# A Mamba recurrence that begins with four input projections done instead of six, and makes five a step instead of three

## The reference

```
zxbcdt = x @ in_proj_w.T            # z 1024 | xv 256 | B 256 | C 1024 | dt_in 128
dt  = softplus(dt_in @ dt_proj_w.T + dt_proj_b)        # 1024 channels
dA  = exp(dt[..., None] * A);  dBx = (dt * x_full)[..., None] * Bg   # 16 states each
h_t = dA_t * h_(t-1) + dBx_t ;  y_t = sum over states of C_t * h_t
y   = (y + D_skip * x_full) * silu(z)  ->  out_proj
```

## Time and profile before

| | us |
|---|---|
| median of 3 runs | 2858.53 (2854.5 to 2859.29) |
| the profiled execution | 2856.02 |
| its span | 2854.2 |
| VectorE, TensorE, POOL, ScalarE busy in it | 2129.0, 2650.3, 1256.3, 1152.0 |
| first scan of step 0 begins | 77.13 |

### The profile page before, as it was taken

The page is one execution under the profiler, slowest core; times in us unless marked ns, Lnnn a source line. Parts: engine busy times, 40 slices in busy tenths (PEclk is TensorE's granted clock), DMA queues, the critical chain, the costliest instruction groups (busy, mean ns, idle before and its releaser), DMA issues.

```text
span 2854.2 us, 32450 instructions
## 1 busy us (share of the span) xinstructions
PE 2650.3 (93%) x11096; PEld 1884.4 (66%) x11096; DVE 2129.0 (75%) x2731; ACT 1152.0 (40%) x1690; POOL 1256.3 (44%) x836
## 2 busy tenths in 40 slices
PE   7888888888888878999999999999999999999999
PEld 3444444444444327888887777888877888888887
DVE  4999999999999985653366677778767865556553
ACT  5555555555455534432244443443333422222221
POOL 2789888988889971210000023223312522222220
PEclk8888998989889869999999999999999999999999
DMA  6654654554465527221111112112111121111111
GB/s 232 210 158 119 188 163 122 151 174 126 120 192 149 149 82 244 94 74 49 48 67 60 45 37 67 45 45 67 45 38 45 45 52 45 52 49 48 51 46 67
DMA packets 152309, 275.35 MB, mean 96 GB/s; under 512 B 27344, under 2 KB 27856, under 8 KB 151632
## 3 DMA queue, kind: packets, MB, share of 16 engines
q1 hardware_dynamic: 152144, 273.27, 32.3%
HBM read 178.01 MB, written 61.34 MB: 84 GB/s over the span
## 4 chain that ended last, share of the span: by engine, by line
PE 70%; DVE 11%; ACT 8%; issue 4%; POOL 3%; DMA 2%; SPq 1%; DVEq 0%; POOLq 0%; ACTq 0%
PE ps L1733 18%; PE ps L1734 18%; PE ps L1735 18%; PE ps L1772 8%; DVE state L1358 5%; ACT ps L847 5%; PE ps L1784 4%; POOL read L1172 2%; DMA vpack<-vl 1%; PE ps L1924 1%; DVE act_o L1677 1%; PE ps L1868 1%; DMA uraw<-y_d 1%; PE ps L1898 1%; DVE drive L1349 1%
## 5 line engine op out<-in xcount | busy, mean ns | idle before, releaser
L1172 POOL TENSOR_TENSOR read<-state,c_t 128x512 f32<-128x512 f32 x512 | 664.3, 1310 | 134.9 <-DVE state L1358 115.9
L1358 DVE TENSOR_TENSOR_SCAN state<-ps,drive 128x512 f32<-128x512 f32 x512 | 624.8, 1220 | 13.1 <-ACT ps L847 11.5
L1733 PE MATMUL ps<-xh,ghi 128*128 128x512 f32 x1536 | 608.3, 396 | 0.0
L1231 POOL TENSOR_TENSOR wdeq<-packed,scales 128x1024 f32<-128x1024 f16 x96 | 260.3, 2711 | 789.1 <-DVE packed L1510 789.1
L1735 PE MATMUL ps<-xh,glo 128*128 128x512 f32 x1536 | 599.0, 390 | 0.0
L1734 PE MATMUL ps<-xl,ghi 128*128 128x512 f32 x1536 | 598.7, 390 | 0.0
L847 ACT ACTIVATE ps<-ps,a_exp 128x512 f32<-128x512 f32 x512 | 338.8, 662 | 470.6 <-PE ps L1772 468.9
L1772 PE MATMUL ps<-dpack,sel 128*128 128x512 f32 x512 | 261.4, 511 | 110.7 <-DVE state L1358 109.3
L1677 DVE TENSOR_TENSOR act_o<-act_o,ps 128x512 f32<-128x512 f32 x192 | 131.7, 686 | 306.1 <-PE ps L1735 290.3
L1349 DVE TENSOR_TENSOR drive<-ps,b_t 128x512 f32<-128x512 f32 x512 | 346.3, 676 | 11.9 <-PE ps L1772 11.4
L1099 ACT ACTIVATE ahi<-act_o 128x512 fp32r<-128x512 f32 x192 | 121.4, 632 | 562.2 <-DVE act_o L1677 562.2
(11 more groups left out here) (204 smaller groups left out, 3782.6 us busy)
## 6 DMA issues: line engine op xcount, KB each, us to landing
whi<-w_d SPq DMA_DIRECT2D x63, 256.0 KB, 4.1
wlo<-w_d SPq DMA_DIRECT2D x63, 256.0 KB, 4.9
dpack<-dh SPq DMA_DIRECT2D x64, 128.0 KB, 3.8
dpack<-dl SPq DMA_DIRECT2D x64, 128.0 KB, 3.5
b_d<-ev SPq DMA_DIRECT2D x32, 256.0 KB
x_d<-ev SPq DMA_DIRECT2D x32, 256.0 KB, 2.6
vpack<-vh SPq DMA_DIRECT2D x64, 128.0 KB, 3.4
vpack<-vl SPq DMA_DIRECT2D x64, 128.0 KB, 2.6
```

Source lines behind the costliest of these rows:

```text
L1172: pool.tensor_tensor(read[:, n % RRING, :], state[:, n % SRING, :], c_t[:, g % 2, :], ALU.mult).then_inc(read_ready, 1)
L1231: pool.tensor_tensor(wdeq[:, :].rearrange("p (h n) -> p h n", h=2), codes, scale, ALU.mult).then_inc(deq, 1)
L1358: dve.tensor_tensor_scan(state[:, n % SRING, :], ps[:, n % 2, :], drive[:, n % DRING, :], 0.0, ALU.mult, ALU.add)\
L1733: pe.matmul(out_, w_h, x_h, start=(start and k == 0), stop=False)
```

## The change

Four jobs are done before step 0, then five in each of the steps 0 to 15, each over three states (blocks 0, then 1, then 2 and 3); steps 16 to 31 hold none. The norm of batch 3 and the end of that of batch 2 are written into step 0. `scale_x` is in steps 1, 5, 9 and the splits in 2, 6, 10. Since a batch's dt tile is now computed steps before its use, it is spilled and loaded back (`load_dt_in`, `take_dt`) in steps 6, 14 and 22. SP's order is rewritten accordingly. `sp_rest` shares its memory with `sp_abs`, which makes room for `dt_in`.

```diff
+LEAD_JOBS, STEP_JOBS = 4, 5
+DT_STEP = tuple(CT * b - 2 for b in range(B))
+SCALE_STEP, SPLIT_STEP = (None, 1, 5, 9), (None, 2, 6, 10)
-MEAN_BANK, VAR_BANK = (0, 2, 0, 2), (1, 3, 1, 4)
+MEAN_BANK, VAR_BANK = (0, 2, 0, 4), (1, 3, 4, 4)
...
+    sp_rest = place("sp_rest", [P, S], F32, offset_of["end"] - 4 * S)
-    sp_rest = place("sp_rest", [P, S], F32, after())
+    dt_in = place("dt_in", [P, S], F32, after())
...
 
         def step_jobs(g):
 
-            nb, k = divmod(g + 2, CT)
-            return nb, k, nb < B and k < IN_TILES // 3
-
-        def spills(tile):
-            return 0 if tile == 0 else 4 if tile in (X0, B0, X1, B1) else 1
+            first = LEAD_JOBS + STEP_JOBS * g
+            return first, max(0, min(STEP_JOBS, IN_TILES * B - first))
+
+        def slot_of(c):
+
+            return divmod(c, 3) if c < 3 * STEP_JOBS else (STEP_JOBS, 0)
+
+        def spills(job):
+            return 0 if job == 0 else 4 if job % IN_TILES in (X0, B0, X1, B1) else 1
...
+            sp.dma_start(mean_w[:, :], t["mean_w"]).then_inc(mean_loaded, 16)
             for f in range(FT):
                 sp.dma_start(xlr[0][:, f, :], t["x"][:, f, cols(0)]).then_inc(x0_loaded[f], 16)
-                if f == 0:
-                    sp.dma_start(mean_w[:, :], t["mean_w"]).then_inc(mean_loaded, 16)
...
+                elif tile == 0:
+                    dsts = [dt_d[:, cols(nb)]]
...
+            def load_dt_in(nb):
+                job = IN_TILES * nb
+                sp.wait_ge(spilled[job % 3], spill_count(job))
+                if nb >= 2:
+                    sp.wait_ge(dtlo_ready, nb)
+                sp.dma_start(dt_in[:, :], dt_d[:, cols(nb)]).then_inc(dt_in_loaded, 16)
...
@@ -600,24 +614,29 @@
             store_hat(0)
             store_w(2)
             copy_x0()
+            spill(B0)
+            store_w(3)
             load_pack_dt(0)
-            spill(B0)
+            load_b(0)
+            load_pack_v(0)
             spill(X0)
-            load_pack_v(0)
-            load_b(0)
-            store_w(3)
+            store_w(4)
             spill(3)
-            store_w(4)
             load_c(0)
             load_x(1)
             store_w(5)
-            spill(4)
-            store_w(6)
-            store_w(7)
-            spill(5)
...
+                first, jobs = step_jobs(g)
...
-                if 0 <= g + 1 < STEPS:
+                if g + 1 in DT_STEP[1:]:
+                    load_dt_in(DT_STEP.index(g + 1))
+                if more:
                     load_b(g + 1)
-                if jobs:
-                    weights_after(first)
-                    spill(first)
-                if 0 <= g + 1 < STEPS:
+                weights(0)
+                keep(0)
+                if more:
                     load_c(g + 1)
+                weights(1)
                 if g >= 1:
                     store_y(g - 1)
-                if jobs:
-                    weights_after(first + 1)
-                if 0 <= g + 1 < STEPS:
+                keep(1)
+                weights(2)
+                if more:
                     load_pack_dt(g + 1)
+                keep(2)
+                if more:
                     load_pack_v(g + 1)
-                if jobs:
-                    spill(first + 1)
+                weights(3)
+                keep(3)
                 if g + 2 < STEPS:
                     load_x(g + 2)
-                if jobs:
-                    weights_after(first + 2)
-                    spill(first + 2)
+                weights(4)
+                keep(4)
...
+            def take_dt(nb):
+                act.wait_ge(dt_in_loaded, 16 * nb)
+                act.wait_ge(dtp_ready, CT * nb)
+                act.activation(dthi[:, :], dt_in[:, :], ACT.Copy).then_inc(dthi_ready, 1)
...
                     act.wait_ge(sp_exp_ready, q)
+                    act.wait_ge(sp_sum_ready, q)
...
             take(0)
-            squares(1)
             take(1)
             soften(0)
-            root_1(1)
             take(2)
             w_high(3)
+            squares(1)
             dt_high(0)
-            root_2(1)
-            squares(2)
+            root_1(1)
             v_high(0)
             w_high(4)
+            squares(2)
+            root_2(1)
             take(3)
             soften(1)
+            w_high(5)
             root_1(2)
-            w_high(5)
-            root_2(2)
-            squares(3)
-            take(4)
-            root_1(3)
-            w_high(6)
-            root_2(3)
-            take(5)
-            w_high(7)
             act.wait_ge(a_ready, 2)
...
+                first, jobs = step_jobs(g)
                 for c in range(NST):
+                    i, part = slot_of(c)
                     decay(g, c)
+                    if g == 0:
+                        if c == 1:
+                            root_2(2)
+                        if c == 4:
+                            squares(3)
+                        if c == 7:
+                            root_1(3)
+                        if c == 9:
+                            root_2(3)
                     for b in (1, 2, 3):
-                        if g == CT * b - 5 and c % 4 == 1:
+                        if g == SPLIT_STEP[b] and c % 4 == 1:
                             split_hi(b, c // 4)
+                        if g == DT_STEP[b] and c == 2:
+                            take_dt(b)
-                    if jobs and c % 4 == 2 and c < 12 and first + c // 4 + 2 < IN_TILES:
-                        w_high(first + c // 4 + 2)
-                    if jobs and c % 4 == 2 and c > 4:
-                        take(first + c // 4 - 1)
+                    if part == 0 and 1 <= i <= jobs:
+                        take(first + i - 1)
+                    if part == 1 and i < jobs and first + i + 2 < IN_TILES:
+                        w_high(first + i + 2)
...
-                dve.tensor_tensor(dtlo[:, :], ps[:, 5 + (IN_TILES * nb) % 2, :],
+                dve.tensor_tensor(dtlo[:, :], dt_in[:, :] if nb else ps[:, 5, :],
...
-            dve.wait_ge(dwhi_ready, 1)
-            dve.tensor_tensor(dwlo[:, :], dwraw[:, :], dwhi[:, :].bitcast(F32), ALU.subtract)\
-               .then_inc(dwlo_ready, 1)
...
-            centre(1)
             w_low(2)
+            dve.wait_ge(dwhi_ready, 1)
+            dve.tensor_tensor(dwlo[:, :], dwraw[:, :], dwhi[:, :].bitcast(F32), ALU.subtract)\
+               .then_inc(dwlo_ready, 1)
             dt_split(0)
             dve.wait_ge(sel_loaded, 32)
             dve.tensor_copy(sel[:, :, :], selraw[:, :, :]).then_inc(sel_ready, 1)
             dve.wait_ge(a_ready, 1)
             dve.tensor_scalar(a_exp[:, :], a_exp[:, :], -1.0, None, ALU.mult).then_inc(a_ready, 1)
+            centre(1)
             soft_rest(0)
+            w_low(3)
             hat_variance(1)
-            w_low(3)
             centre(2)
             both_roots(1)
             w_low(4)
-            soft_rest(1)
-            hat_variance(2)
-            w_low(5)
-            centre(3)
-            both_roots(2)
-            hat_variance(3)
-            w_low(6)
-            both_roots(3)
-            w_low(7)
...
+                    if g == 0:
+                        if c == 0:
+                            soft_rest(1)
+                        if c == 1:
+                            hat_variance(2)
+                        if c == 2:
+                            w_low(5)
+                        if c == 3:
+                            both_roots(2)
+                        if c == 4:
+                            centre(3)
+                        if c == 7:
+                            hat_variance(3)
+                        if c == 10:
+                            both_roots(3)
-                        if g == CT * b - 6 and c % 4 == 1:
+                        if g == SCALE_STEP[b] and c % 4 == 1:
                             scale_x(b, c // 4)
-                        if g == CT * b - 5 and c % 4 == 2:
+                        if g == SPLIT_STEP[b] and c % 4 == 2:
                             split_lo(b, c // 4)
+                        if g == DT_STEP[b] and c == 5:
+                            dt_split(b)
-                    if jobs and c % 4 == 3 and c < 12 and first + c // 4 + 2 < IN_TILES:
-                        w_low(first + c // 4 + 2)
-                    if nb and jobs and k == 0 and c == 6:
-                        dt_split(nb)
-                    if nb < B and c == 15:
+                    if part == 2 and i < jobs and first + i + 2 < IN_TILES:
+                        w_low(first + i + 2)
+                    if g + 2 < STEPS and c == 15:
...
-                        if b >= 2:
-                            pe.wait_ge(ln_centred, FT * (b - 1))
+                        if b == 2:
+                            pe.wait_ge(ln_centred, FT)
+                        if b == 3:
+                            pe.wait_ge(ln_u, 3)
...
-                if b == 2:
-                    pe.wait_ge(ln_u, 1)
```

(62 more changed lines are left out.)

14 lines of the change are left out of this document (5 added, 9 removed).

## The result

The changed kernel takes 2863.3 us (median of 9 runs, 2861.1 to 2868.1), the kernel before, measured beside it, 2855.6 us (9 runs, 2850.0 to 2859.7). The ratio is 1.0026 with a 95% interval of 1.0015 to 1.0036: a little slower, where 2843 was forecast. Its profiled execution took 2862.3 us, for which my sum gave 2841.1.

The account below looks back on a forecast made before the run. The recurrence was taken as a VectorE chain with a 28.7 us step floor, plus lead-in and TensorE stalls above it. -8.0 + 2.9 - 9.8 = -14.9 on 2856.0 gave 2841.1, as a median 2843; range 2832 to 2858.

Parts of the forecast that it names:

- Part 1: Lead-in before the recurrence: projections and norm work leave it, first scan at 56 us instead of 77.1, range 54 to 61.
- Part 2: Step 0: 38.6 us of VectorE work plus 6.5 us of stall, 45 us; step 1 begins 8.0 us earlier, at 101.0.
- The second pass: Step 0, variance of batch 3: holds spread_dt(6) on TensorE, hidden mostly under centre's 2.4 us on VectorE.
- Part 3: Steps 1 to 15, five tiles each: 29.2 us per step plus extras, 471.2 us against 468.3, +2.9 us.
- the extras: Steps 1 to 15: scale and split 22 us, ten w_low 8, dt_split twice 1.2, steps 12 and 13 1 each.
- rival A: Steps with projections: more transfers make the v pack late, about 2 us more, 15 times, 2873 us; chance 0.10.
- the price of 1 us each for steps 12 and 13: Added because their first or second tiles are B or X, with four spills ahead of the packs.
- Theory Q: Posed for the experiments, not in the prediction: weights are late, issued behind an X or B tile's fourfold spill with too little lead.
- Part 4: Steps 16 to 31, without projections: fourteen at 29.45 us, then 29.6 and 28.4; 470.9 against 480.7, -9.8 us.
- rival C: Steps without projections stay at half clock throughout, state 12 stalls in each: 14 x 0.73 = +10, 2853 us; chance 0.10.
- B: TensorE's clock still falls at the step's end, state 1 loses 25.4 us as now: +14.7, 2858 us; chance 0.10.

Follow-up runs that it names:

- e8: e5 with the lead-in's first C tile spilled and loaded ahead of X0's four spills; 2842.6 us, 0.9949 of the kernel before.
- e5: e1 with POOL's normalise one step later for batch 2 and three steps later for batch 3; 2844.4 us, 0.9956 of the kernel before.
- e1: Changed kernel with only SP's order altered: from step 3 on, weights are issued ahead of the spills; 2847.8 us, 0.9973 of the kernel before.
- e2: Changed kernel with each X and B tile spilled once instead of four times, loads reading that one copy; 2842.1 us, 0.9951 of the kernel before.
- e3: Changed kernel's lead-in, but four tiles a step over four states each, weights(2) and keep(1) ahead of the v pack; 2867.2 us, 1.0040.
- e6: e3 with both packs ahead of weights(2) and later spills, and norm work of batches 2 and 3 in later steps; 2854.0 us, 0.9988.
- e9: e8 with the spill of an X or B tile in second place moved behind the v pack; 2853.2 us, 0.9984 of the kernel before.
- e10: Lead-in, norms and six leading tiles of the kernel before; five tiles a step in e5's order, keep(2) behind the packs; 2860.9 us, 1.0016.

## Why the prediction was wrong, step by step

**Part 1, right.** First scan at 55.88 for a forecast of 56, and by the chain that was forecast: ScalarE ends root_1(2) at 55.2 (54.9 in the sum), and its decay follows without a gap.

**Part 2, too small by 4.4 us.** Step 0 took 49.45 us, not 45. The term that was mis-sized is the price of two passes of eight matmuls, the column means and the variance of batch 3: 3.5 and 3.6 us, by the row at 45.84 in the earlier trace rows. They took 5.37 and 5.40. The order of time shows both, the waits behind them, and two w_low (columns as in the earlier trace rows; TensorE, ScalarE, VectorE, POOL):

```profile
60.86 5.37 PE L1753 MATMUL ps<-xlr,mean_w 128*128 128x512 f32 x8 [3.20 <-DVE selraw L1331]
...
75.03 5.40 PE L1762 MATMUL ps<-xhr,mean_w 128*128 128x512 f32 x8 [4.38 <-ACT xhr L772]
...
68.12 0.66 ACT L873 ACTIVATE ps<-ps,a_exp 128x512 f32<-128x512 f32 x1 [4.92 <-PE ps L1809]
...
64.44 3.50 DVE L1353 TENSOR_TENSOR wlo<-wraw,whi 128x512 fp32r<-128x512 f32 x2
...
82.08 0.69 DVE L1378 TENSOR_TENSOR drive<-ps,b_t 128x512 f32<-128x512 f32 x1 [3.46 <-PE ps L1809]
...
61.97 1.27 POOL L1201 TENSOR_TENSOR read<-state,c_t 128x512 f32<-128x512 f32 x1 [11.29 <-DMA c_t<-c_d]
```

Each pass began after TensorE had stood, for 3.20 and 4.38 us, and the windows view shows a granted clock of 0.50 within each:

```profile
61.80:65.10 3.30, 3.30 (x5) 1.35 (x4) 1.80 (x2) 1.40 (x3) 3.13 (x3) 0.50 0.05 20
75.50:78.80 3.30, 3.30 (x5) 1.35 (x4) 1.89 (x3) 1.76 (x4) 0.69 (x1) 0.50 0.30 79
```

Behind each stand six projection matmuls and the spreads of the next states: the decay at 68.12 waited 4.92 us for them, and the drive at 82.08 waited 3.46 us. The second pass had been called mostly hidden. The two passes exceed their price by 3.7 us, most of the 4.4; this is read from the order of time, and no experiment took it apart.

VectorE's busy time in step 0, 41.58 us where I had summed 38.6, points elsewhere and misleads. Of the 3.0 us more, 2.3 are the two w_low, 1.2 us by my price and 3.5 beside a POOL that had waited 11.3 us for c_t and was behind. But the drive after them ended at 68.58, and the scan at 68.88 waited for the decay, so they cost nothing; e8 says the same.

**Part 3, the failed step.** It priced a step at 29.2 us and the extras at 33 us. Both were off, in opposite directions: clean steps took 28.7, which is 7 us less over fifteen; and the extras were 39 us, 6 more (491.8 less fifteen floors of 28.72 and 22 us of late weights). That the two cancel is luck, and so in part is that e5 does the stretch in 471.9 us for a forecast of 471.2; e5 still has some 5 us of delay in steps 4, 12, 13 and 14. What made the forecast fail is the sentence, written against rival A, that "weights' loads have five or more states of lead", with the price of 1 us each for steps 12 and 13. Three buffers and slots of three states give six states, 10.3 us at 1.71, from a buffer's release to its use; slots of four gave eight, 13.7 us. That is enough for a load alone, which lands in 4.7 us in the median, not for one that first stands 3.3 us in issue behind B's spill and is then usable 6 to 9 us later. Two readings could have told: the spill's own landing of 6.3 us in the earlier trace rows, which I used for the lead-in and not here, and the landing of the weights' own loads in the kernel before, up to 6.7 us, which I did not ask for. I looked for the late transfer at the v pack, which had waits in the earlier trace rows, and looked at no queue position of the weights. Theory Q is shown by e1, where the order alone took 20.0 us out of the four steps, by e2, and by e3 (steps 11 and 15), e6, e9 and e10, which moved the place of the loss with whatever they put behind the spill. Why the loads behind a B tile's spill landed later than those behind an X tile's in the changed kernel was not tested.

**Part 4, right.** 470.7 us for 470.9, at a granted clock of 0.72 over these steps. The gather of state 12 in step 21 takes 1.06 us (at 764.99), as forecast; rival C, half clock throughout, did not come, and neither did B: the clock in steps 3, 7, 11 and 15 is 1.00.

**Rival A** had the right sign and the wrong object: its transfers came late in four steps by 1 to 8 us, not in fifteen by 2. Forecast 2841.1 plus 4.3 for step 0, 20.6 for steps 1 to 15, less 0.2 and 3.6 for the rest, is 2862.2, against 2862.3 measured.

Mended stalls uncover others. Of the 20.0 us that e1 takes out of steps 4, 8, 12 and 13, 4.7 come back in step 5, since a VectorE that no longer waits finds POOL behind.

## What to carry to other kernels

When slots of a pipeline get shorter, work out anew the lead of everything that is loaded per slot, as buffers times slot length, and set it against issue plus landing of the largest thing that stands ahead on the same queue. A row that prices such a transfer once holds everywhere that it stands in the queue. Moving one transfer ahead of another pays where the one that moves back has time to spare (e1: 20.0 us out, about 2 back in the packs); where it has none, it only chooses who is late (e6, e9, e10). And an engine's busy time that exceeds the sum is not yet the cause: ask what the next instruction on the path waited for.

## What the runs showed of the hardware

A weight pair (two loads of 256 KB) issued behind the B tile's spill of four times 256 KB was usable 8.8 us after the issue of its second load in the changed kernel's step 12, and 6.5, 6.1 and 5.9 us after it in its step 4, in e6 and in e10; behind an X tile's spill of as many bytes in the changed kernel the same load landed in 4.4 to 5.1 us, over all of steps 1 to 15 in 4.7 us in the median, and a v pack in steps without projections lands in 2.2 to 2.4 us. The issues on SP's queue grew too: 1.2 to 1.5 us for each of those loads, against 0.45 in the median.

Scale_x, a VectorE instruction with its inputs in SBUF, took 0.72 to 1.6 us in e5, and 6.42 us in e1 and e2 beside a POOL that was 3.3 us behind. Behind is not enough: w_low, with its inputs in SBUF too, took 1.8 us at most beside a POOL that was up to 4.2 us behind. Drives and scans, which take one input from PSUM, never took more than 0.69 and 1.23 us in e1.

TensorE's granted clock stayed at 1.00, its upper level of 2.4 GHz, through steps with projections up to state 14, one thin state included. After an idle of 6.0 us in step 12 the gather ran at the lower level, 1.2 GHz (1.94 us against 1.06), and after 3.2 and 4.4 us in step 0 the eight matmuls of a norm took 5.4 us, against 3.6.
